# GpSimd's place for the division of the exponentials: between the two additions of a step, or behind the inverse square roots

## What is computed

```python
def _layer(x, wqkv, qs, ksc, wo, lg, lb, w1, b1, w2, b2):
    h = shift_token(x)
    q, k, v = jnp.split(h @ wqkv, 3, axis=-1)      # 8 heads of 64
    q = l2norm(q) * qs                             # each head's vector by its length
    k = l2norm(k) * ksc
    q, k = rotary_xpos(q, k)
    o = local_attention(q, k, v)                   # windows of 64, keys of the own and the last window
    x = x + o @ wo
    h = shift_token(x)
    h = (h - mu) / jnp.sqrt(var + 1e-05) * lg + lb
    a, g = jnp.split(h @ w1 + b1, 2, axis=-1)
    return x + (a * jax.nn.gelu(g)) @ w2 + b2

# in local_attention
attn = jax.nn.softmax(jnp.where(mask, -big, sim), axis=-1)
out = jnp.einsum('bhwij,bhwjd->bhwid', attn, bv)
```

## Time and profile before

| | |
|---|---|
| median of 3 runs | 1432.54 us (1431.04 to 1433.38) |
| the profiled execution, own time | 1430.35 us |
| its span in the trace | 1428.5 us |
| TensorE busy | 1258.4 us, 88% |
| VectorE busy | 1262.2 us, 88% |
| ScalarE busy | 943.0 us, 66% |
| GpSimd busy | 905.3 us, 63% |

### The profile page before, as it was taken

The page is one execution under the profiler, slowest core; times in us unless marked ns, Lnnn a source line. Parts: engine busy times, 40 slices in busy tenths (PEclk is TensorE's granted clock), DMA queues, the critical chain, the costliest instruction groups (busy, mean ns, idle before and its releaser), DMA issues.

```text
span 1428.5 us, 36014 instructions
## 1 busy us (share of the span) xinstructions
PE 1258.4 (88%) x12288; PEld 984.8 (69%) x12288; DVE 1262.2 (88%) x2418; ACT 943.0 (66%) x1708; POOL 905.3 (63%) x787
## 2 busy tenths in 40 slices
PE   5889989998889898997789889898988999999985
PEld 3667767777667676775567777677776777777764
DVE  4999999999999999997688888888888899988974
ACT  3566666566666566564478777777877778787772
POOL 0733443344433443346798888888888899999972
PEclk8899999999999999999899999999999999999999
DMA  5000000000000000000111111121111211212111
GB/s 167 1 10 13 12 5 10 11 11 11 9 11 11 11 2 11 8 8 12 36 43 45 41 41 40 39 49 35 44 41 45 55 45 46 49 42 55 43 32 33
DMA packets 87051, 44.14 MB, mean 31 GB/s; under 512 B 43908, under 2 KB 80176, under 8 KB 86960
## 3 DMA queue, kind: packets, MB, share of 16 engines
q1 hardware_dynamic: 86960, 42.95, 12.0%
HBM read 19.86 MB, written 6.29 MB: 18 GB/s over the span
## 4 chain that ended last, share of the span: by engine, by line
DVE 45%; issue 19%; POOL 17%; PE 16%; DVEq 1%; ACT 1%; POOLq 0%; DMA 0%; SPq 0%; ACTq 0%
DVE sums L1004 9%; DVE probs L1036 7%; POOL rnorm L660 7%; DVE mx L1030 5%; POOL kT L668 4%; PE bank L1389 3%; POOL kT L649 3%; DVE xo L1065 2%; DVE hc L1102 2%; DVE qT L1084 2%; PE bank L1376 2%; PE bank L1473 2%; PE bank L1445 2%; DVE f_sum L1184 2%; DVE conv L947 1%
## 5 line engine op out<-in xcount | busy, mean ns | idle before, releaser
L625 POOL TENSOR_TENSOR probs<-probs,coef 128x1024 f32<-128x1024 f32 x128 | 239.5, 1901 | 201.0 <-DVE coef L996 201.0
L796 ACT ACTIVATE probs<-probs 128x1024 f32<-128x1024 f32 x128 | 134.8, 1053 | 98.8 <-DVE probs L1036 98.2
L649 POOL TENSOR_TENSOR kT<-qT 128x512 f32<-128x512 f32 x128 | 162.7, 1272 | 53.8 <-DVE qT L1084 53.6
L660 POOL TENSOR_TENSOR rnorm<-norm,halves 128x16 f32<-128x16 f32 x64 | 188.9, 2952 | 6.1 <-POOL norm L657 1.5
L1291 PE MATMUL bank<-ident,probs 128*128 128x128 f32 x1024 | 144.0, 286 | 49.2 <-POOL probs L625 49.2
L783 ACT ACTIVATE wT<-bank 128x512 f32<-128x512 f32 x256 | 138.6, 596 | 63.8 <-PE bank L1291 62.8
L1030 DVE TENSOR_REDUCE mx<-bank 128x8 f32<-128x512 f32 x256 | 164.0, 682 | 14.3 <-PE bank L1304 12.9
L1036 DVE TENSOR_TENSOR probs<-bank,mx 128x512 f32<-128x512 f32 x256 | 163.7, 682 | 0.0
L1291 PEld LDWEIGHTS bank<-ident,probs 128*128 128x128 f32 x1024 | 116.2, 145 | 68.3 <-POOL probs L625 57.4
L1304 PE MATMUL bank<-kT,qT 64*128 64x256 f32 x1024 | 157.2, 429 | 5.4 <-DVE probs L1036 5.4
L1004 DVE TENSOR_REDUCE sums<-probs 128x16 f32<-128x1024 f32 x128 | 153.4, 1211 | 0.0
(11 more groups left out here) (120 smaller groups left out, 3097.8 us busy)
## 6 DMA issues: line engine op xcount, KB each, us to landing
probs<-f_v SPq DMA_DIRECT2D x96, 128.0 KB, 2.3
res<-stage_x SPq DMA_DIRECT2D x48, 128.0 KB, 3.8
xn<-in_x SPq DMA_DIRECT2D x16, 128.0 KB, 2.2
xr<-in_x SPq DMA_DIRECT2D x16, 128.0 KB, 2.1
stage_x<-xo SPq DMA_DIRECT2D x32, 64.0 KB, 1.6
hn<-stage_x SPq DMA_DIRECT2D x32, 64.0 KB
mn<-mid SPq DMA_DIRECT2D x64, 32.0 KB
stage_x<-yo SPq DMA_DIRECT2D x16, 128.0 KB, 2.1
```

The costliest lines, as they stand in the source:

```text
L625: nc.gpsimd.tensor_tensor(out=e[:, :, :, :], in0=e[:, :, :, :], in1=coef[r][:, 2, A_REP * ng:A_REP * (ng + 1), :].unsqueeze(3).broadcast_t ...
L649: nc.gpsimd.tensor_tensor(out=qk[m][:, :, :], in0=on_self[m % 2][:, :, :], in1=on_partner[m % 2][:, :, :], op=ALU.add).then_inc(added, 1)
L660: nc.gpsimd.tensor_tensor(out=rnorm[:, at], in0=norm2[:, 1, at], in1=halves[:, 0:2 * F_HEADS], op=ALU.pow).then_inc(rnorm_set, 1)
```

## The change

On GpSimd the division is written behind `inverse_norms`; before, it was written between the two calls of `sums`. The wait for the inverses of the sums (`f_rsum_set`) goes with it. Nothing is added and nothing removed, and the lists of the other engines stay as they are.

```diff
                         if prepares(turn, p):
                             sums(4 * (unit + 1) + 2 * tile, 2 * tile)
+                        local = f_late(turn, s, "stats")
+                        if local is not None:
+                            rstd_of(mmv[local % PAIR], mrstd[local % PAIR], m_eps, m_rstd, m_stats, PAIR * it + local)
+                        if prepares(turn, p):
+                            sums(4 * (unit + 1) + 2 * tile + 1, 2 * tile + 1)
+                            inverse_norms(unit + 1, tile)
                         if f_exists(turn, s):
                             e = fE[s % F_RING].rearrange("p k a n -> p (k a) n")[:, 0:F_HEADS - F_NORM_ACT, :]
                             inverse = f_rsum[s % 2][:, :, :].rearrange("p k a -> p (k a)")[:, 0:F_HEADS - F_NORM_ACT]
                             pool.wait_ge(f_rsum_set, n + 1)
                             nc.gpsimd.tensor_tensor(out=e, in0=e, in1=inverse.unsqueeze(2).broadcast_to([P, F_HEADS - F_NORM_ACT, F_KEYS]),
                                                     op=ALU.mult).then_inc(f_normed, 1)
-                        local = f_late(turn, s, "stats")
-                        if local is not None:
-                            rstd_of(mmv[local % PAIR], mrstd[local % PAIR], m_eps, m_rstd, m_stats, PAIR * it + local)
-                        if prepares(turn, p):
-                            sums(4 * (unit + 1) + 2 * tile + 1, 2 * tile + 1)
-                            inverse_norms(unit + 1, tile)
```

## The result

The changed kernel takes 1585.3 us (median of 4 runs, 1584.1 to 1590.1) against 1432.2 us: the ratio is 1.1075, with an interval of 1.105 to 1.1101, so 153 us slower. The forecast was 1563 us and the range 1530 to 1605. The profiled execution took 1590.13 us, 5 us above the median, with a span of 1588.3 us and a mean granted clock of 0.924 (0.972 before).

What follows compares the result with a forecast made beforehand. A circle through GpSimd, TensorE, ScalarE and VectorE was taken to bind the changed kernel: 1430.35 us plus 112 gives 1542, and 21 for TensorE's lowered clock makes 1563 us. The range was 1530 to 1605 us.

Steps and rivals of the forecast that it cites:

- its slack: Time from the division's end to the transposes needing it: 3.5 us; the end was to move by 6.6 us.
- A circle through four engines: Division, transposes, copies, exponential, sum, second rotation, second addition, power, division: 13.65 us in odd steps, 12.29 in even.
- the competitor: Path over TensorE to the maxima and down VectorE's list to the sum: 15.89 us against 16.46 by the loop.
- Its length at full clock, 25.94 us per pair: Loop summed over an odd and an even step, against 22.31 to 22.5 us before the change.
- The path through the exponential: Transposes to ScalarE's copies and exponential, then VectorE's sum: 3.08 us odd or 1.72 even, plus 1.09.
- a sign of being wrong: VectorE waiting for the scores instead of the exponential would mean the competitor wins and TensorE sets the price.
- The clock, priced at +21 us within 0 to 88: TensorE's idling in each step brings half clock: 0.7 us taken per pair, from 0 to 2.9 possible.
- On the loop itself lie only the transposes: Of TensorE's work only the transposes, 1.03 us, stretch the loop at half clock: 0 to 0.9 us per step.
- Priced in full in every step: Rival: TensorE's clock falls fully in every step, 1542 + 88 = 1630 us; chance 0.12.
- Insertion alone: Rival: no loop closes; the division adds 1.34 us between power and scaling in odd-to-even passages, 1471 us; chance 0.09.
- Not slower: Rival: GpSimd saves 37.4 us idling ahead of the division, 1393 us, if its end moves under 3.5; chance 0.04.
- The clock at full: Rival: the loop closes and TensorE's clock stays at full, 1542 us; chance 0.18.

Runs made afterwards that it cites:

- experiment 1: Changed kernel with GpSimd's division directly behind the second addition but ahead of the floor and power: 1474.98 us, ratio 1.0306.
- the cheap power: A multiplication replaces GpSimd's power -0.5, norms left out of the output: changed kernel 1398.53 us, kernel before 1372.22 us.
- experiment 3: Changed kernel with ScalarE's exponential ahead of its two copies and TensorE's output product ahead of the transposes: 1495.27 us, ratio 1.0459.
- filled kernel: Changed kernel with ten more TensorE products, mask by identity, ahead of its wait for the division: 1535.18 us, ratio 1.0737.
- experiment 2: Changed kernel with ScalarE's exponential ahead of its two copies of the transposes: 1576.74 us, ratio 1.1019.
- experiment 5: Changed kernel with ScalarE's exponential ahead of its copies and ten filling products on TensorE ahead of its wait: 1520.79 us, ratio 1.0626.
- experiment 4: The run of the filled kernel, against the changed kernel: 1535.18 us, ratio 1.0737.
- the split power: Kernel before, with floor and power taken per block, the first block's directly behind the first addition on GpSimd: 1415.32 us, ratio 0.99.

## Why the prediction was right, and where it was off

- *The division costs nothing where it stood, and its end moves by more than its slack.* Right. In the kernel before the transposes wait for it nowhere. They wait 152.5 us for it in the changed kernel; experiment 1, with a division that is in time, has nearly none.
- *A circle through four engines closes.* Shown from two sides: at GpSimd (experiment 1, -110 us; the cheap power, -187) and at ScalarE and TensorE with GpSimd's list left alone (experiment 3, -90, which also shortens the competitor by moving the output product off it).
- *Its length at full clock, 25.94 us per pair, and 1542 us.* The filled kernel measures 25.62 us and 1535 us. The difference is 0.16 us per step, 10 us over 61. The terms hold one by one. In the filled kernel, averaged over the even steps from 8 to 60 and the odd ones from 7 to 61, division to transposes takes 1.31 us (predicted 1.34), transposes to sum 2.76 and 4.18 (2.81 and 4.17), sum to second addition 3.60 and 3.50 (3.54), second addition to division 4.50 and 4.47 (4.6).
- *The path through the exponential.* Right in length, incomplete as a map. The output product with L1167, and in odd steps the values' product with L1110, run beside it within a few tenths of a us per step. Cutting the path that the prediction named wins 9 us (experiment 2) or 14 (experiment 5), and the table load in it is worth 8, not 36. The competitor was named, and lies where it was put: it binds once the exponential's path is cut (experiments 3 and 5). That VectorE waits for the scores was listed as a sign of being wrong, and it does so for 108.6 us in the changed kernel, more than for the exponential. But it waits for them in the kernel before as well, and what decides is the last wait ahead of the second addition, at L1167, L1184 or L1110. In the eight odd steps where none of these waits, such as 25, the sum still stands 4.2 us behind the transposes, as in the filled kernel.
- *The clock, priced at +21 us within 0 to 88.* Mis-sized: it is 50 us, by experiment 4, or 27.33 - 25.62 = 1.7 us per pair of steps where 0.7 was taken. The figure that failed is "On the loop itself lie only the transposes". The output product lies on it too, since the sum stands behind L1167, so in step 24 the half clock stretches the path from transposes to sum from 2.81 to 4.17 us, 1.36 where at most 0.9 was allowed. In odd steps so does the values' product, for which L1110 waits. The length of the half level, taken as 3.4 us from the earlier trace rows, did not fail: it was 6.8 us in step 24, but a mean clock of 0.90 makes 120 of the 600 us from 750 to 1350, an estimate of 2.7 us for each of the 44 steps in them.
- *Where the 50 us lie* can be read by comparing the changed kernel with the filled one, again over the steps 7 to 61. From division to division an even step takes 12.83 us on average in place of 12.16, an odd one 14.51 in place of 13.46. Between transposes and sum are 0.60 us of that in even steps and 0.47 in odd ones; 0.57 lie between sum and second addition in odd steps.
- *The Trainium skill's advice against idle gaps on TensorE* (TensorE: Matmul & The Clock Gate, "Why this matters for your kernels") named the right danger, and the filled kernel shows its price. The trace agrees in part: the half clock comes behind a gap of 3.07 us in step 24, but also behind 2.53 us in step 21 and 2.29 us in the earlier trace rows, shorter than those the advice speaks of, and it stays away behind 3.04 us in step 20. Priced in full in every step it would have been 1630 us, 45 too much.
- *The rivals.* Insertion alone, 1471 us, is what experiment 1 measures, 1475; in the changed kernel it isn't alone. "Not slower" needed a move of under 3.5 us. The clock at full, 1542 us, is the filled kernel.

Two errors partly cancel in the forecast's distance of 22 us, which is luck: the circle came out 7 us shorter than summed, and the clock 29 us dearer. What stays open is which idle times bring the half clock. The intervals between divisions vary from 12.2 to 15.0 us with it, and no run here tells why step 20 was spared and step 21 was not.

## What to carry to other kernels

When an instruction is moved behind others on its engine, don't stop at who waits for it: follow its consumers down their own lists until they come back to one of the instructions it now stands behind. If they do, the step time is the length of that circle, and it can be summed from rows before the change; an idle gap ahead of an instruction is a reason to leave it there, or to put more work in, as the split power did. And where several queues carry the same lateness, cutting one of them shows little: experiment 2 alone would have cleared the circle of blame.

## What the hardware showed that I had not expected

- Ten products per step that compute nothing made the changed kernel 50 us faster (1585.3 to 1535.2), by the granted clock's rise from 0.90 to 1.00.
- The half clock can outlast the gap that it comes with: some 6.8 us at the half level around an idle time of 3.07 us in step 24. It does not come with every gap: none around 3.04 us in step 20.
- GpSimd's power goes with its columns only in part: 0.71 us for 2, 1.67 for 8, 2.93 for 16.
